# Two of nine interpolation taps transposed by DMA, and sampling one tile later

## The chip, the cores and the metric

The kernel runs on one core of one Trainium2 chip. The metric is the device time of one execution in microseconds; the median of three runs of the kernel before is 2494.78 us (2494.53 to 2497.68).

## The reference

The input is x with shape [4, 128, 64, 64] in float32. Layer 0 is a group norm, an attention over the 4096 pixels of each image with 128 channels, a projection and a residual. Layer 1 is

```python
out = relu(batchnorm(conv2d(x, w1)))              # 3x3
offsets = conv2d(out, w_off) + b_off              # 18 channels: 9 rows, 9 columns
# for each pixel and each of the 9 taps: position = pixel + tap + offset, clipped
# value = bilinear mix of the 4 neighbours of that position
out = batchnorm(conv2d(sampled values, w2))       # one 128x128 matrix per tap
return relu(out + x)
```

## The kernel before, in words

The program is written by hand with one instruction stream per engine and semaphores between them. Helpers: `after(eng, key, n)` waits until the semaphore `key` has counted n steps, and `stored` waits for n transfers of 16 counts. A number in float32 is carried as a sum of two float16 numbers (hi and lo), and `three` (lines 1039 to 1043) makes a product of three float16 matmuls: hi by hi (line 1041), hi by lo (1042) and lo by hi (1043). The attention stage (until about 1600 us of the span) already transposes part of its probabilities by DMA: line 264 issues one transfer of twelve 128x128 blocks per step on the queue of the SyncE engine (SP). Then come conv1, the offset conv (lines 1177 to 1209), and the deformable stage, which the change is about.

The deformable stage works on 128 tiles of 128 pixels (4 images of 32 tiles, a tile is eight patches of 4x4 pixels). `HALF` = 16 tiles make a half image, and TensorE's loop body (line 1265) is one half image. A tile q goes through these steps:

- GpSimd (`interp`, line 451) multiplies row weights and column weights ("hats") into SS, 128 pixels by nine taps by 120 window positions, in float32. SS has two buffers. Its wait is for the transposes of the tile two before.
- TensorE (`interp_transposes`, line 1217) transposes the nine taps, three each into PSUM banks 0 to 2, waiting for VectorE to have emptied the bank.
- ScalarE (`interp_hi`, line 623) copies each bank to STh in float16, laid out patch by patch with the taps side by side, and VectorE (`interp_lo`, line 975) subtracts it from the bank into STl. Both have two buffers.
- SP (line 309) loads for every second tile a window of h1 (`XW`, four buffers) in three transfers of 320 KB, each 10 rows by 4 by 8 KB.
- TensorE (`sample`, line 1225) multiplies for each of the eight patches the window by the weights, three matmuls of 144 columns a patch, in sections of three, three and two patches (banks 3 to 5).
- ScalarE (`sampled`, line 631) and VectorE (`sampled_lo`, line 982) split the result in hi and lo.
- TensorE (`conv2`, line 1237) multiplies it by the weights of the nine taps, 27 matmuls of 128 columns, and VectorE adds it to the output (`z_add`) and takes statistics every fourth tile.

In one turn of TensorE's loop the order is: transposes of tile q, then a section of `sample` for tile q-1 and a third of `conv2` for tile q-2, three times. In tiles 5 and 8 of a half image GpSimd also computes the distances for the next half image (`distances`), and in tiles 10 to 13 ScalarE turns them into hats (`hats`, line 641), between the copies of `interp_hi` and `sampled`. The order on each engine is fixed by the program.

Of the kernel before, what the change touches and what calls it, by code (L numbers as in the profile page):

```python
# [18 lines left out]
F16 = mybir.dt.float16  # L19
I32 = mybir.dt.int32  # L20
ALU = mybir.AluOpType
# [19 lines left out]
TAPS = 9  # L41
# [21 lines left out]
NBUF = 4  # L63
SECT = ((0, 3), (3, 3), (6, 2))
# [30 lines left out]
def build(nc, x, weights, consts, out):  # L95
# [6 lines left out]
    with ctx:  # L102
# [3 lines left out]
        def sb_in(scope, name, shape, dt):  # L106
# [46 lines left out]
        XS = sb_in(l1, "xt_stage", [128, 2, 4, 2 * C], F16)  # L153
        l1a = ExitStack()
        ZT = sb_in(l1a, "zeros_f16", [128, 768], F16)
# [22 lines left out]
        STh = sb_in(l1b, "interpT_hi", [128, 2, 8, TAPS, 16], F16)  # L178
        STl = sb_in(l1b, "interpT_lo", [128, 2, 8, TAPS, 16], F16)
# [29 lines left out]
        s_ld = [sem(f"windows_loaded{i}") for i in range(NBUF)]  # L209
        s_fx = [sem(f"final_loaded{i}") for i in range(B)]  # L210
# [13 lines left out]
            tt="interp_transposed", th="interpT_hi_ready", tl="interpT_lo_ready", mm="sampled",  # L224
# [18 lines left out]
        def _(sp):  # L243
# [57 lines left out]
            for i in range(2):  # L301
                stored(sp, s_xs[i], B * NCH * 2)
            after(sp, "l1", L1_FLAG)
# [5 lines left out]
            with sp.Fori(0, ny) as iy:  # L309
                with sp.Fori(0, nx) as ix:  # L310
                    with sp.Fori(0, B) as b:
                        for i in range(HH // TW):

                            after(sp, "mm", (iy * SX + ix) * (3 * GROUPS) + b * (3 * GPI) + 6 * (i - (NBUF - 1)))
                            row = (iy + sy0) * WR + b * IMG_ROWS + (GUARD + TW * i - 3 - WR * (SY // 2))
                            slot = row * PITCH + (ix + sx0) * (WC // TW) + (0 - (WC // TW) * (SX // 2))
                            for a in range(WC // TW):
                                src = bass.AP(xt_dram.tensor, (slot + a) * (2 * C),
                                              [[PITCH * 2 * C, WR], [SLOTS * 2 * C, TW], [1, WW // TW * 2 * C]])
                                sp.dma_start(XW[WR * TW * a:WR * TW * a + WR * TW, i % NBUF, :, :], src).then_inc(s_ld[i % NBUF], 16)  # L320
# [11 lines left out]
        def _(po):  # L332
            for k in s:
                po.sem_inc(s[k], OPEN)
            for k in s_xo + s_xs + s_tr:
                po.sem_inc(k, OPEN)
# [93 lines left out]
            po.tensor_tensor(SM[:, 12:13], SM[:, 11:12], SM[:, 0:1], ALU.pow).then_inc(s["l1p"], 1)  # L430
            for b in range(B):
# [929 lines left out]
```

## Time and profile before

| what | value |
|---|---|
| median of three runs | 2494.78 us |
| profiled execution | 2493.83 us |
| its span, first to last instruction | 2491.7 us |
| PE (TensorE) busy | 2315.7 us, 93% |
| DVE (VectorE) busy | 1855.8 us, 74% |
| ACT (ScalarE) busy | 1795.1 us, 72% |
| POOL (GpSimd) busy | 1310.9 us, 53% |
| granted TensorE clock over the span | 0.97 |
| first transpose of the deformable stage | 1886.26 us |
| last sampled subtraction of the stage | 2444.47 us |

Busy shares are averages over stages. For the deformable stage the rows below give its own pace. PE is TensorE's matmuls, PEld its weight loads, SPq the queue of SP; L1222 is line 1222.

### The profile page before, as it was taken

To read this page: it belongs to the slowest core of one execution; us is meant where nothing else is said; L and a number is where in the kernel's file an instruction comes from. 1 tells how busy PE (TensorE), PEld (TensorE's weight loads), DVE (VectorE), ACT (ScalarE), POOL (GpSimd) and SP (SyncE) were. 2 spreads that over 40 slices of the span, in tenths; PEclk is the share of its full clock that TensorE was granted. 3 is DMA by queue.
4 is the path that set the end of the run, shared out by engine and by line. 5 is a ranking of instruction groups with operands and counts; after the bars stand their busy time and mean duration, and the time that the engine had idled before them with its cause. 6 is when DMAs were issued, how large, how long until landed. Compare 5 with 4: busy or idle time off the path is not lost.

```text
span 2491.7 us, 73903 instructions
## 1 busy us (share of the span) xinstructions
PE 2315.7 (93%) x27053; PEld 1877.2 (75%) x27053; DVE 1855.8 (74%) x3901; ACT 1795.1 (72%) x2963; POOL 1310.9 (53%) x1067
## 2 busy tenths in 40 slices
PE   5999999999999999999999999799877999899992
PEld 3777777777777777777777777588447999899992
DVE  6778777778877777877777777587666877777875
ACT  5778888878888888888888888532556766666754
POOL 4557545555545555544555555663116665556650
PEclk9999999999999999999999999899898999999996
DMA  3878887778787877877777777771224433333336
GB/s 108 166 144 147 141 162 140 147 149 146 145 159 133 150 145 145 150 129 129 149 147 146 148 146 148 192 235 59 66 71 133 124 113 113 111 111 117 115 95 270
DMA packets 917462, 345.25 MB, mean 139 GB/s; under 512 B 844256, under 2 KB 904160, under 8 KB 909024
## 3 DMA queue, kind: packets, MB, share of 16 engines
q1 hardware_dynamic: 917216, 341.87, 63.6%
q8 instruction: 167, 2.74, 0.5%
q14 instruction: 79, 0.65, 0.1%
HBM read 98.76 MB, written 41.68 MB: 56 GB/s over the span
## 4 chain that ended last, share of the span: by engine, by line
PE 75%; issue 9%; POOL 7%; DVE 4%; DMA 3%; ACT 1%; SPq 1%; POOLq 0%; DVEq 0%; ACTq 0%
PE psum L1041 14%; PE psum L1042 14%; PE psum L1043 14%; POOL probs_split L363 7%; PE psum L1080 7%; PE psum L1082 7%; PE psum L1081 7%; PE psum L1222 5%; PE psum L1066 3%; DMA probsT_dma<-probs_split 1%; PE psum L1195 1%; DMA final<-x_scratch 1%; DVE padded_hi L946 0%; PE psum L1120 0%; PE psum L1203 0%
## 5 line engine op out<-in xcount | busy, mean ns | idle before, releaser
L363 POOL TENSOR_TENSOR probs_split<-probs,probs_split 128x768 f16<-128x768 f32 x512 | 841.8, 1644 | 697.0 <-ACT probs_split L512 696.8
L711 DVE TENSOR_REDUCE neg_max<-psum 128x1 f32<-128x1024 f32 x512 | 626.6, 1224 | 333.0 <-PE psum L1043 332.8
L509 ACT ACTIVATE probs<-psum,exp_bias 128x1024 f32<-128x1024 f32 x512 | 570.2, 1114 | 220.2 <-DVE exp_bias L713 215.6
L1080 PE MATMUL psum<-vT_hi,probsT_dma 128*128 128x129 f16 x3072 | 549.6, 221 | 4.1 <-DMA probsT_dma<-probs_split 4.1
L1082 PE MATMUL psum<-vT_hi,probsT_dma 128*128 128x129 f16 x3072 | 549.5, 219 | 0.0
L1081 PE MATMUL psum<-vT_lo,probsT_dma 128*128 128x128 f16 x3072 | 549.4, 218 | 0.0
L512 ACT ACTIVATE probs_split<-probs 128x768 f16<-128x768 f32 x512 | 431.7, 843 | 22.8 <-ACT probs L509 1.0
L455 POOL TENSOR_TENSOR interp<-row_hats,col_hats 128x360 f32<-128x360 f32 x384 | 294.4, 795 | 219.6 <-PE psum L1222 214.7
L1041 PE MATMUL psum<-k_hi,q_hi 128*128 128x512 f16 x1024 | 387.8, 379 | 3.9 <-DVE q_lo L827 2.4
L1042 PE MATMUL psum<-k_lo,q_hi 128*128 128x512 f16 x1024 | 388.1, 379 | 0.0
L1043 PE MATMUL psum<-k_hi,q_lo 128*128 128x512 f16 x1024 | 388.1, 379 | 0.0
L1081 PEld LDWEIGHTS psum<-vT_lo,probsT_dma 128*128 128x128 f16 x3072 | 302.2, 98 | 0.0
L1080 PEld LDWEIGHTS psum<-vT_hi,probsT_dma 128*128 128x128 f16 x3072 | 297.6, 97 | 5.0 <-DMA probsT_dma<-probs_split 4.9
L1082 PEld LDWEIGHTS psum<-vT_hi,probsT_dma 128*128 128x128 f16 x3072 | 296.1, 96 | 0.0
L980 DVE TENSOR_TENSOR interpT_lo<-psum,interpT_hi 120x384 f16<-120x384 f32 x384 | 191.3, 550 | 89.5 <-ACT interpT_hi L629 88.5
L638 ACT ACTIVATE sampled_hi<-psum 128x432 f16<-128x432 f32 (+1 forms) x384 | 182.3, 495 | 90.0 <-PE psum L1043 89.8
L988 DVE TENSOR_TENSOR sampled_lo<-psum,sampled_hi 128x432 f16<-128x432 f32 (+1 forms) x384 | 207.1, 553 | 51.2 <-ACT sampled_hi L638 46.7
L629 ACT ACTIVATE interpT_hi<-psum 120x384 f16<-120x384 f32 x384 | 162.4, 491 | 92.2 <-PE psum L1222 89.9
L723 DVE TENSOR_TENSOR probsT_lo<-psum,probsT_hi 128x256 f16<-128x256 f32 x512 | 214.0, 418 | 3.1 <-ACT probsT_hi L502 3.1
L1041 PE MATMUL psum<-sampled_hi,weights_hi 128*128 128x128 f16 x1152 | 215.5, 221 | 0.6 <-DVE sampled_lo L988 0.6
L1043 PE MATMUL psum<-sampled_hi,weights_lo 128*128 128x128 f16 x1152 | 214.1, 220 | 0.0
L1042 PE MATMUL psum<-sampled_lo,weights_hi 128*128 128x128 f16 x1152 | 213.8, 220 | 0.0
(181 smaller groups left out, 5532.1 us busy)
## 6 DMA issues: line engine op xcount, KB each, us to landing
xt_windows<-xt_scratch SPq DMA_DIRECT2D x192, 320.0 KB
xt_scratch<-zeros_f SPq DMA_DIRECT2D x28, 576.0 KB, 4.4
probsT_dma<-probs_split SPq DMA_TRANSPOSE x512, 3.7
x_residual<-x SPq DMA_DIRECT2D x128, 64.0 KB, 2.6
x_scratch<-x_out SPq DMA_DIRECT2D x128, 64.0 KB, 2.4
x_rows<-x_scratch SPq DMA_DIRECT2D x32, 256.0 KB, 3.4
xt_scratch<-xt_stage SPq DMA_DIRECT2D x128, 64.0 KB
final<-x_scratch SPq DMA_DIRECT2D x16, 512.0 KB, 10.7
```

The source lines that it names most:

```text
L363: po.tensor_tensor(PH[:, j, 1, :], P[:, j, 0:DW], PH[:, j, 0, :], ALU.subtract).then_inc(s["pl"], 1)
L455: last = po.tensor_tensor(SS[:, g % 2, :, WR * TW * a:WR * TW * a + WR * TW].rearrange("p k (j x) -> p k j x", j=WR), HX[:, hb, g, :, :, N ...
L509: act.activation(P[:, j, :], sc, ACT.Exp, bias=NB[:, par, j:j + 1]).then_inc(s["exp"], 1)
L512: act.activation(PH[:, j, 0, :], P[:, j, 0:DW], ACT.Copy).then_inc(s["ph"], 1)
L711: ve.tensor_reduce(NM[:, par, j:j + 1], sc, AX.X, ALU.max, negate=True).then_inc(s["mx"], 1)
L723: ve.tensor_tensor(PTl[:, k, :, :].rearrange("p m q -> p (m q)"), PS[:, 4 + j % 2, 0:CH - DW], PTh[:, k, :, :].rearrange("p m q -> p (m q) ...
L1041: pe.matmul(dst, lh, rh, start=start, stop=False)
L1042: pe.matmul(dst, lh, rl, start=False, stop=False)
L1043: return pe.matmul(dst, ll, rh, start=False, stop=stop)
L1080: pe.matmul(dst, th, Vh[:, p, v, 0:129], start=n == 0, stop=False)
L1081: pe.matmul(dst[:, 0:128], th, Vl[:, p, v, :], start=False, stop=False)
L1082: last = pe.matmul(dst, tl, Vh[:, p, v, 0:129], start=False, stop=n == KT - 1)
```

## The change

The interpolation taps 0 to 6 are transposed by TensorE, four into PSUM bank 0 and three into bank 1, and copied out by ScalarE and VectorE bank by bank. The taps 7 and 8 don't pass TensorE: ScalarE copies them from SS to SH in float16 (`dma_taps_hi`), VectorE subtracts that from SS (`dma_taps_lo`), and SP transposes the four blocks (two taps, hi and lo, 120 columns padded to 128) with one DMA to the buffer ST that TensorE reads. ST keeps each tap as hi and lo blocks of 128 pixels, and has four buffers in place of two; SH has four. A sample matmul therefore reads its 144 moving columns as nine runs of 16. Sampling of a tile comes two tiles behind its transposes, conv2 three tiles, z_add four. GpSimd's `interp` waits for the VectorE split as well. On SP the two transposes of a tile pair stand between the window loads, and the first image of a pass is written out ahead of the loop over images. The padding of SH is cleared once by GpSimd before the stage, and XS (a buffer of the stage before) moves to make room.

```diff
+DTAP = 2
+PTAP = ((0, 4), (4, 3))
+T0 = TAPS - DTAP
-        STh = sb_in(l1b, "interpT_hi", [128, 2, 8, TAPS, 16], F16)
-        STl = sb_in(l1b, "interpT_lo", [128, 2, 8, TAPS, 16], F16)
+        ST = sb_in(l1b, "interpT", [128, 4, TAPS, 2, 128], F16)
 # SP
+                    def transposed(b, g):
+                        q = (iy * SX + ix) * GROUPS + b * GPI + g
+                        after(sp, "dl", q + 1)
+                        after(sp, "mm", q * 3 - 9)
+                        sp.sem_inc(s_go, 1)
+                        sp.dma_start_transpose(ST[:, g % 4, T0:TAPS, :, :].rearrange("p k e x -> p (k e) x"),
+                                               SH[:, g % 4, :, :, :].rearrange("p k e x -> p (k e x)")).then_inc(s_td[g % 4], 16)
+                    def image_steps(b, first):
                         for i in range(HH // TW):
+                            windows(b, i)
+                            if i or not first:
+                                transposed(b, 2 * i - 2)
+                                transposed(b, 2 * i - 1)
 # GpSimd, interp
-                after(po, "tt", q * 3 - 3)
+                after(po, "tt", q * 2 - 2)
+                after(po, "dl", q - 1)
 # ScalarE
+            def dma_taps_hi(q, g, hid):
+                after(act, "pr", q + 1)
+                stored(act, s_td[g % 4], hid * 4 + g // 4)
+                act.activation(SH[:, g % 4, :, 0, 0:KW], SS[:, g % 2, T0:TAPS, :], ACT.Copy).then_inc(s["dh"], 1)
...
-                        for i in range(3):
+                        dma_taps_hi(q, g, hid)
+                        for i in range(2):
                             interp_hi(q, g, i)
...
-                                sampled(q - 1, (g + 1) % 2, i)
+                                sampled(q - 2, g % 2, i)
 # VectorE
+            def dma_taps_lo(q, g):
+                after(ve, "dh", q + 1)
+                ve.tensor_tensor(SH[:, g % 4, :, 1, 0:KW], SS[:, g % 2, T0:TAPS, :], SH[:, g % 4, :, 0, 0:KW], ALU.subtract).then_inc(s["dl"], 1)
...
+                            dma_taps_lo(q0 + g, g)
+                            for i in range(2):
+                                interp_lo(q0 + g, g, i)
 # TensorE
-                for i in range(3):
-                    after(pe, "tl", q * 3 + (i - 2))
-                    for k in range(3):
-                        last = pe.transpose(PS[0:KW, i, 128 * k:128 * k + 128], SS[:, g % 2, 3 * i + k, :], ident)
+                for i, (k0, nk) in enumerate(PTAP):
+                    after(pe, "tl", q * 2 + (i - 1))
+                    for k in range(nk):
+                        last = pe.transpose(PS[0:KW, i, 128 * k:128 * k + 128], SS[:, g % 2, k0 + k, :], ident)
                     last.then_inc(s["tt"], 1)
...
+                    sh, sl = (ST[0:KW, g % 4, :, e, 16 * t:16 * t + 16] for e in range(2))
+                    dst = PS[:, 3 + i, 144 * (t - t0):144 * (t - t0) + 144].rearrange("p (k x) -> p k x", k=TAPS)
+                    last = three(dst, xw[:, 0:C], xw[:, C:2 * C], sh, sl, True, True)
...
-                                sample(q - 1, p, i)
-                            if g >= 2 or not first:
-                                conv2(q - 2, g % 2, i)
+                                if i == 0:
+                                    pe.wait_ge(s_td[p % 4], (hid * 4 + ((g - 2) // 4 + 1)) * 16 + OPEN)
+                                sample(q - 2, p, i)
+                            if g >= 3 or not first:
+                                conv2(q - 3, (g + 1) % 2, i)
```

## Rows read from the trace of the kernel before

**Rows 1.** The page's head, the span.
```profile
span 2491.7 us, 73903 instructions
```

**Rows 2.** Who TensorE waited for, 1885 to 2455: total us, times, longest.
```profile
PE psum L1222 <- issue: 30.1, 6, 6.6
PE psum L1222 <- POOL interp L455: 14.9, 1, 14.9
```

**Rows 3.** Chain of waits, 1900 to 2492: start us, us, what.
```profile
2088.23 2.17 PE psum L1222 x9
2098.72 0.99 PE psum L1222 x9
2106.73 0.99 PE psum L1222 x9
...
2154.77 6.65 issue
```

**Rows 4.** Timeline, one tile from 2102.56: start, us, engine, line, op, count, [idle before].
```profile
2102.56 1.15 PE L1222 MATMUL psum<-constants,interp 128*120 128x128 f32 x9
2102.70 0.46 DVE L988 TENSOR_TENSOR sampled_lo<-psum,sampled_hi 128x288 f16<-128x288 f32 x1 [0.15 <-ACT sampled_hi L638]
2103.17 1.25 ACT L629 ACTIVATE interpT_hi<-psum 120x384 f16<-120x384 f32 x3 [0.50 <-PE psum L1222]
...
2103.55 0.23 PE L1041 MATMUL psum<-interpT_hi,xt_windows 120*128 120x144 f16 x1
...
2103.79 2.30 POOL L455 TENSOR_TENSOR interp<-row_hats,col_hats 128x360 f32<-128x360 f32 x3 [1.70 <-PE psum L1222]
...
2104.11 0.22 PE L1041 MATMUL psum<-sampled_hi,weights_hi 128*128 128x128 f16 x1
```

**Rows 5.** Timeline of ScalarE, VectorE, TensorE in a tile with hats, 1994 to 1998.
```profile
1994.36 1.75 ACT L647 ACTIVATE col_hats<-col_hats,small 128x1728 f32<-128x1728 f32 x1
1995.98 1.26 ACT L638 ACTIVATE sampled_hi<-psum 128x432 f16<-128x432 f32 x3
...
1996.56 1.49 DVE L988 TENSOR_TENSOR sampled_lo<-psum,sampled_hi 128x432 f16<-128x432 f32 x3 [1.12 <-ACT sampled_hi L638]
...
1998.18 0.22 PE L1041 MATMUL psum<-sampled_hi,weights_hi 128*128 128x128 f16 x1
```

**Rows 6.** Groups by line and shape, 1885 to 2455: total us, mean ns, idle before.
```profile
L988 DVE TENSOR_TENSOR sampled_lo<-psum,sampled_hi 128x288 f16<-128x288 f32 x128 | 58.2, 455 | 15.3 <-ACT sampled_hi L638 15.3
L638 ACT ACTIVATE sampled_hi<-psum 128x288 f16<-128x288 f32 x128 | 53.4, 417 | 34.8 <-PE psum L1043 34.8
```

**Rows 7.** DMA queues and issues, 1920 to 2430.
```profile
DMA packets 8639, 57.34 MB, mean 112 GB/s; under 512 B 1710, under 2 KB 1710, under 8 KB 1710
...
q1 hardware_dynamic: 8550, 56.04, 36.1%
...
xt_windows<-xt_scratch SPq DMA_DIRECT2D x171, 320.0 KB
```

**Rows 8.** DMA queues and issues in attention, 400 to 600; last number us to landing.
```profile
q1 hardware_dynamic: 112179, 29.14, 79.3%
...
probsT_dma<-probs_split SPq DMA_TRANSPOSE x69, 3.7
```

**Rows 9.** Line 264 on the SP queue: duration ns min/median/max.
```profile
L264 SPq DMA_TRANSPOSE probsT_dma<-probs_split x64: 1274/1434/2412, 1001.1 to 1199.9; - x64
```

**Rows 10.** Busy time 1877.5 to 1903.5: PE PEld DVE ACT POOL, clock, DMA share, GB/s.
```profile
1877.50:1903.50 26.00, 17.14 (x205) 16.64 (x205) 12.88 (x27) 16.04 (x29) 18.71 (x22) 0.73 0.61 191
```

**Rows 11.** Weight loads of lines 1185 and 1203: ns min/median/max.
```profile
L1185 PEld LDWEIGHTS psum<-constants,h_rows x128: 195/209/231, 1745.4 to 1860.5; 128*128 128x128 f32 x128
...
L1203 PEld LDWEIGHTS psum<-constants,offset_rows x128: 138/140/231, 1755.7 to 1864.4; 128*128 128x128 f32 x128
```

**Rows 12.** Timeline of GpSimd, and chain of waits, at the start of the stage.
```profile
1883.82 9.27 POOL L455 TENSOR_TENSOR interp<-row_hats,col_hats 128x360 f32<-128x360 f32 x12 [4.78 <-ACT col_hats L650]
...
1896.70 0.98 PE psum L1222 x9
```

More of the change, by code:

```diff
@@ L209, in build @@
         s_ld = [sem(f"windows_loaded{i}") for i in range(NBUF)]
+        s_td = [sem(f"interp_dma_transposed{i}") for i in range(4)]
+        s_go = sem("interp_transpose_released")
         s_fx = [sem(f"final_loaded{i}") for i in range(B)]
@@ L302, in _ @@
                 stored(sp, s_xs[i], B * NCH * 2)
+            sp.wait_ge(s_pz, 11)
             after(sp, "l1", L1_FLAG)
@@ L310, in _, with windows @@
                 with sp.Fori(0, nx) as ix:
-                    with sp.Fori(0, B) as b:
-                        for i in range(HH // TW):
[L314 to L320, printed above, removed]
+                    def windows(b, i):
+                        after(sp, "mm", (iy * SX + ix) * (3 * GROUPS) + b * (3 * GPI) + 6 * (i - (NBUF - 1)))
+                        row = (iy + sy0) * WR + b * IMG_ROWS + (GUARD + TW * i - 3 - WR * (SY // 2))
+                        slot = row * PITCH + (ix + sx0) * (WC // TW) + (0 - (WC // TW) * (SX // 2))
+                        for a in range(WC // TW):
+                            src = bass.AP(xt_dram.tensor, (slot + a) * (2 * C),
+                                          [[PITCH * 2 * C, WR], [SLOTS * 2 * C, TW], [1, WW // TW * 2 * C]])
+                            sp.dma_start(XW[WR * TW * a:WR * TW * a + WR * TW, i % NBUF, :, :], src).then_inc(s_ld[i % NBUF], 16)
@@ L321, in _ @@
+                    image_steps(0, True)
+                    with sp.Fori(1, B) as b:
+                        image_steps(b, False)
+                    transposed(B - 1, GPI - 2)
+                    transposed(B - 1, GPI - 1)
             for i in range(4 * B):
@@ L334, in _ @@
                 po.sem_inc(s[k], OPEN)
-            for k in s_xo + s_xs + s_tr:
+            for k in s_xo + s_xs + s_tr + s_td:
                 po.sem_inc(k, OPEN)
@@ L672, in _ @@
                 half_image(NHALF - 1, 1, False, True)
-                for i in range(3):
-                    sampled(n * GROUPS + (GROUPS - 1), 1, i)
+                for g in range(2):
+                    for i in range(3):
+                        sampled(n * GROUPS + (GROUPS - 2 + g), g, i)
             after(act, "l1", L1_AB2)
@@ L1008, in half_image @@
                         if g < HALF:
-                            for i in range(3):
-                                interp_lo(q0 + g, g, i)
-                        if 3 <= g < HALF + 3:
-                            z_add(q0 + (g - 3), h, g - 3)
-                        elif g < 3 and not first:
-                            z_add(q0 + (g - 3), h - 1, g - 3 + HALF)
-                        if g <= HALF and (g or not first):
-                            for i in range(3):
-                                sampled_lo(q0 + (g - 1), (g + 1) % 2, i)
+                            dma_taps_lo(q0 + g, g)
+                            for i in range(2):
+                                interp_lo(q0 + g, g, i)
+                        if 4 <= g < HALF + 4:
+                            z_add(q0 + (g - 4), h, g - 4)
+                        elif g < 4 and not first:
+                            z_add(q0 + (g - 4), h - 1, g - 4 + HALF)
+                        if g < HALF + 2 and (g >= 2 or not first):
+                            for i in range(3):
+                                sampled_lo(q0 + (g - 2), g % 2, i)
                         if g >= 4 and g % 4 == 3:
@@ L1227, in sample @@
                 if i == 0:
-                    after(pe, "tl", q * 3 + 3)
+                    after(pe, "tl", q * 2 + 2)
                 after(pe, "xl", q * 3 + (i - 2))
```

40 lines of the change are left out of this document (19 added, 21 removed).

## The prediction

> **What bounds the kernel now.** I read the views in this order: who TensorE waited for in the deformable stage, the chain that ended last, one tile of the timeline, one of the tiles in which ScalarE also prepares weights ("hats"), then the DMA queues. The span is 2491.7 us [rows 1]; the stage runs from about 1886 to 2445, 128 tiles. In all of it TensorE waited only 14.9 us for the first interp tile and 30.1 us in six stalls with no releaser ("issue") [rows 2]. The stalls (5.0 us in the mean, up to 6.65) lie at the jumps back of TensorE's loop over half images, and behind each the nine transposes take 2.17 instead of 0.99 us [rows 3]. Between them TensorE is never idle: two tiles take 2106.73 - 2098.72 = 8.01 us, 4.00 each. A tile is 0.99 us of nine transposes (2102.56 to 2103.55), 24 sample matmuls in three pieces, the first piece of nine 0.56 us (to 2104.11), and 27 conv2 matmuls; these 51 take the other 3.01 us [rows 4]. ScalarE's copies, VectorE's subtractions and GpSimd's products (2.30 us of 4.00, then idle 1.70) run in its shadow. So the stage is TensorE's count of instructions times their pace; what leaves TensorE leaves the time, until something in its shadow comes out.
>
> **Part 1, the transposes.** Nine transposes a tile become seven. Each takes 0.99 / 9 = 0.110 us [rows 3], so the tile falls by 0.22 us to 3.78; 128 x 0.22 = **-28.2 us**. The bank waits fall from three a tile to two and are not waited on now [rows 2].
>
> **Part 2, copies of the seven taps.** ScalarE and VectorE handle 512 + 384 columns in two instructions instead of 3 x 384 = 1152 in three, and add one each of 240 columns out of SBUF: 1136 columns, again three instructions. The nearest rows to 240 columns are those of 288, 0.417 us on ScalarE and 0.455 on VectorE [rows 6]; 48 columns fewer are a little less, I take 0.37 and 0.40. Bounds 0.3 and 0.6. Total load is unchanged. The new split of the two taps can run at the tile's start, where ScalarE now idles 0.50 us before its first copy [rows 4]; VectorE waits there too. Cost nothing in ordinary tiles. If VectorE and GpSimd slowed each other here, GpSimd's 1.70 us of idle (1.48 at the new period) covers it. GpSimd's new wait (for the split of the tile two before) is passed about 1.2 us into the tile, where its old one (2103.79 - 2102.56 = 1.23) was [rows 4]; behind it only interp and the distances queue, and TensorE needs the result a whole tile later.
>
> **Part 3, tiles with hats.** In four of 16 tiles ScalarE puts a hat (up to 1.75 us) between the interp copies and the sampled copies. There the shadow is full: the last subtraction ends at 1996.56 + 1.49 = 1998.05 and conv2 reads it at 1998.18 [rows 5]; 0.13 us to spare. Counted from that tile's start (1992.63), the subtraction ends at 5.42. After the change the first copy starts 0.11 later (four transposes, not three, ahead of it), two copies take some 0.25 less than three, so it ends near 5.28; conv2 wants it at 3.78 + 0.77 + 0.56 = 5.11. It is 0.2 to 0.3 late, and the next tile's first copy is up to 0.28 later again, behind the new split. The two column hats pay, the shorter row hats hardly: 0.4 us in each of seven half images with hats, **+3 us** (bounds 0 and 7: nothing, or 0.25 in all 28 such tiles).
>
> **Part 4, the transfer.** Per tile one DMA transpose of four 128x128 blocks. The nearest row is attention's, of twelve blocks (line 264): 79.3% of 16 engines for 200 us is 2538 engine-us for 69 transfers and some copies, about 35 each without the copies; landing 3.7 us after issue [rows 8]. A third is 12 engine-us, 0.75 us over 16 engines. Bounds: 0.7 (a third) and 2.2 us (as much as twelve blocks). Its issue on the SP queue takes at most the 1.43 us of twelve blocks [rows 9]; SP is otherwise idle.
> The windows: 15 transfers took the 26 us of the row, 1.73 each, at 0.61 of 16 engines [rows 10]. The 1710 small packets of 171 transfers are ten for each [rows 7], so each runs on ten engines; 36.1% x 16 x 510 / 171 = 17.2 engine-us over ten is again 1.7. Three per two tiles are 5.2 us. With two transposes 5.2 + 1.5 = 6.7 of 7.56 us: busy, not binding.
> The Trainium skill (DMA: Bandwidth & Descriptors, "Why a DMA increments its semaphore by 16 and not by 1") says that the engine count of a hardware-issued DMA is the largest number up to 16 that divides the slowest dimension of both sides; the window's is ten rows, so ten engines. By that rule the trace agrees, and the transposes, with 128 partitions, would use all 16.
> Latency: the split is ready some 1.2 us into tile q, sampling needs it at 2 x 3.78 + 0.77 = 8.3, so 7.1 us are there. The worse of two transposes is issued one tile behind a window (5.2 us, about 1 us before it starts), lands some 8 us after that window's issue, which is 4.2 to 4.5 us after its own. Slack near 3 us: **0**. The windows' own requests move behind the transposes in SP's order and then come three tiles after a buffer is free, still five tiles before use: 0. SP's new jump between images can hold one transfer back by a stall as in rows 3, and TensorE's own stall lies on the same spot: 0.
>
> **Part 5, the strided moving operand.** Sampling now reads 9 runs of 16 elements, 512 bytes apart, not 144 in a row. The trace has no such matmul. Weight loads show a strided read: the one with every element 16 bytes apart takes 209 ns against 140 [rows 11], 0.54 ns a jump. Bounds: 0, and 9 x 0.54 = 4.9 ns per matmul, x 24 x 128 = 15 us. I take 0: only one element in 16 is a jump, and row and rule below lean there.
> The Trainium skill (SBUF — State Buffer, the note on cachelines under "Door 1: The DMA port swizzle (why [64,N] ≈ [32,N])") says a read is at full rate if it uses each 16-byte line at least twice; runs of 32 bytes do. By its rule the cost is 0; a reader who takes "each access that crosses to a new line pays" literally gets the 15 us.
>
> **Part 6, ends.** At the start sampling begins a tile later, behind three transposed tiles. GpSimd delivers the first four interp tiles by 1883.82 + 9.27 = 1893.09 [rows 12]; before, by 1896.7 TensorE had done three tiles' transposes and two tiles of sampling [rows 12]. Now three transposed and one sampled are done by 1893.6 to 95, and the missing 3.0 us brings it to 1896.6 to 98: **+1 us** (0 to 2). At the end both orders leave one conv2 alone behind VectorE. The six stalls: the instruction fetch now meets more DMA traffic, and spread by 2 us already: **+1 us** (-5 to +7).
>
> **Sum.** -28.2 + 3 + 1 + 1 = -23.2. Span 2491.7 - 23.2 = 2468.5; the execution adds 2493.83 - 2491.7 = 2.1, 2470.6; the median of the runs, 2494.78, lies 0.95 above the profiled execution: 2471.6. Within 0.2% (5 us) counts as no change.
>
> **Rivals.**
> A, forecast: TensorE-bound tiles of 3.78 us, 2462 to 2481; 0.63.
> B, strided reads cost TensorE up to 4.9 ns a matmul: tile 3.9, gain 8 to 17 us, 2483 in the middle of it. For: rows 11. Against: one jump in 16. 0.13.
> C, the DMA engines become the bound, so TensorE waits for the transposed taps ahead of sampling. Place: ten engines shared by windows and transposes. It decides when 5.2 + 2X exceeds 7.56 (X over 1.2 us) and makes the kernel slower when 5.2 + 2X exceeds 8.0 (X over 1.4). With X = 1.8, between the third and the full row, a tile is 4.4 us: +0.4 x 128 = +51, 2546. For: ten engines at 5.2 us, short packets. Against: attention's 35 engine-us for twelve blocks. 0.12.
> D, the hats and the new order cost more: each late copy moves the next tile (ScalarE's new split queues behind sampled copies, and VectorE, GpSimd behind it). If the shadow holds every tile at about 3.95 us, only 6 us are gained: 2489. For: 0.13 us of margin in hat tiles. Against: in the other 12 of 16 tiles the last subtraction ends at 2102.70 + 0.46 = 2103.16 and conv2 starts at 2104.11 [rows 4], 0.95 us of margin. 0.08.
> E, no gain because the stalls grow by about 4 us each: 6 x 4 eats the gain, 2495. 0.04.
>
> Faster takes A, B, and most of D: 0.81. Same 0.06: E and part of D. Slower 0.13: C and a tail. Range: below A's low end little; C is left out above: 2460 to 2496.
>
> **What would show it.** Right: chain with x7 transposes of 0.77 us every 3.78 us; sample matmuls of unchanged spacing (0.56 us for nine); TensorE waiting for DMA nowhere; waits of 0.2 to 0.4 us on VectorE's sampled subtraction after column hats. Wrong: nine sample matmuls in 0.60 us (B); TensorE waiting for the interp DMA, with issue to landing above 7 us (C); periods of 3.9 us all over with TensorE idle before sampling or conv2 (D); "issue" stalls near 9 us (E).

## The result, and the profile after

The changed kernel takes 2524.66 us (median of four runs, 2520.51 to 2525.37) where the kernel before takes 2494.66 (four runs, 2493.39 to 2497.68): 1.0115 times as long, interval 1.0098 to 1.0133. It is slower by 30 us; the forecast was 2471.6, faster by 23. The profiled execution took 2520.51 us, its span is 2518.5 (2491.7 before, [rows 1]).

Who TensorE waited for in the stage, 1880 to 2480 (total us, times, longest), which answers to [rows 2]. L1261 is the transposes, L1080 the first matmul of three:

```profile
PE psum L1261 <- issue: 40.3, 6, 9.4
PE psum L1080 <- DMA interpT<-interp_split: 17.3, 20, 2.4
PE psum L1261 <- POOL interp L482: 14.9, 1, 14.9
PE psum L1080 <- DVE sampled_lo L1026: 9.0, 13, 1.0
PE psum L1261 <- DVE interpT L1017: 1.7, 2, 0.9
PE psum L1080 <- DVE interpT L1017: 1.7, 1, 1.7
```

Before there were two lines of any size, the stalls at the loop's jumps (30.1) and the first tile (14.9). Now TensorE waits for the new transfer twenty times ahead of sampling, for VectorE thirteen times, and the six stalls are 10 us longer. The chain of waits from 1880 to the end (start us, us, what) shows both at once; its largest share by line is the transfer, 17.0%, and "issue" has 13.3%:

```profile
1984.68 7.78 DMA interpT<-interp_split
...
2012.71 0.77 PE psum L1261 x7
...
2016.50 8.56 issue
2025.06 1.75 PE psum L1261 x7
...
2064.69 11.70 DMA interpT<-interp_split
...
2311.54 9.41 issue
```

The DMA queues and issues of 1920 to 2430, against [rows 7]:

```profile
DMA packets 68737, 70.92 MB, mean 139 GB/s; under 512 B 61923, under 2 KB 61923, under 8 KB 61923
...
q1 hardware_dynamic: 68643, 69.59, 89.2%
...
xt_windows<-xt_scratch SPq DMA_DIRECT2D x167, 320.0 KB
interpT<-interp_split SPq DMA_TRANSPOSE x112, 4.6
```

36.1% of sixteen engines has become 89.2%, for 24% more bytes. One cycle of two tiles, in the timeline (start, us, engine, line, op, count, [idle before]); first TensorE's part of it, then the SP queue's:

```profile
2111.86 0.93 PE L1261 MATMUL psum<-constants,interp 128*120 128x128 f32 x7
...
2115.65 0.93 PE L1261 MATMUL psum<-constants,interp 128*120 128x128 f32 x7
2117.35 0.23 PE L1080 MATMUL psum<-interpT,xt_windows 120*128 120x144 f16 x1 [0.77 <-DMA interpT<-interp_split]
...
2124.16 0.93 PE L1261 MATMUL psum<-constants,interp 128*120 128x128 f32 x7
...
2125.68 0.23 PE L1080 MATMUL psum<-interpT,xt_windows 120*128 120x144 f16 x1 [0.58 <-DMA interpT<-interp_split]
...
2107.50 1.26 SPq L324 DMA_DIRECT2D xt_windows<-xt_scratch  x3
2109.18 4.98 SPq L331 DMA_TRANSPOSE interpT<-interp_split  x2
2114.52 2.29 SPq L324 DMA_DIRECT2D xt_windows<-xt_scratch  x3
2118.39 4.63 SPq L331 DMA_TRANSPOSE interpT<-interp_split  x2
2123.39 1.27 SPq L324 DMA_DIRECT2D xt_windows<-xt_scratch  x3
```

The reader is to see two things. A tile that waits for nothing takes 2115.65 - 2111.86 = 3.79 us, as forecast (3.78); the two that follow take 2124.16 - 2115.65 = 8.51, with a wait of 0.77 us in them for the transfer that was issued at 2109.18. And the even transfer of a pair, the first one behind the windows, is the late one. The next even one, that of the tile of 2115.65, is issued at 2118.39, behind the windows of 2114.52, and lands 7.07 us later, at 2125.46, where TensorE has waited for it since 2125.10. For all 128 the trace gives the issue, and for 96 the landing too:

```profile
L331 SPq DMA_TRANSPOSE interpT<-interp_split x128: 1188/1198/2258, 1890.5 to 2462.2; - x128
...
DMA to landing us min/median/max: 2.4/4.5/11.7
```

Taken apart, the even ones take 7.1 us in the median (32 landings on record), the odd ones 4.1 (64).

Busy time in stretches (PE PEld DVE ACT POOL, clock, DMA share, GB/s): 45 us without a jump, then the three half microseconds in which the transfer issued at 2102.80 runs with the queue to itself, and two stretches in which the queue nearly stands still:

```profile
2102.00:2147.00 45.00, 42.23 (x637) 41.21 (x636) 38.56 (x81) 31.31 (x70) 31.35 (x36) 1.00 0.93 140
...
2104.00:2104.50 0.50, 0.50 (x11) 0.50 (x8) 0.50 (x3) 0.50 (x2) 0.50 (x2) 1.00 0.98 198
2104.50:2105.00 0.50, 0.50 (x7) 0.50 (x6) 0.50 (x3) 0.19 (x1) 0.49 (x1) 1.00 0.31 62
2105.00:2105.50 0.50, 0.50 (x11) 0.49 (x8) 0.50 (x3) 0.48 (x1) 0.00 (x0) 1.00 0.17 33
...
2115.50:2116.70 1.20, 1.08 (x13) 0.84 (x10) 1.05 (x3) 0.87 (x3) 1.20 (x1) 1.00 0.27 26
2123.60:2125.10 1.50, 1.50 (x20) 1.25 (x17) 1.32 (x4) 0.70 (x2) 0.17 (x1) 1.00 1.46 22
```

The same 45 us of the kernel before:

```profile
2102.00:2147.00 45.00, 45.00 (x677) 44.88 (x675) 37.12 (x81) 34.50 (x71) 31.07 (x36) 1.00 0.43 127
```

Alone a transfer is (0.98 + 0.31 + 0.17) x 0.5 x 16 = 11.7 engine-us and lands in 2.4 us: the forecast's 12. TensorE is busy 42.23 us of 45, before in all of them. The last two rows of the first block are not idle time of the queue: by the packet records 23 packets that begin from 2115.3 to 2115.8 end from 2116.7 to 2117.1, and 21 that begin at 2123.7 end at 2125.1; meanwhile 22 to 26 GB/s move, where the 45 us have 140.

**Where the span's 26.8 us lie.** 3.1 lie ahead of the stage (first transpose at 1889.39, before at 1886.26); in the profiled executions of all the kernels below this point lies anywhere from 1884.9 to 1893.1, so these 3.1 need not be the change's. From first to last tile's first transpose it is 571.7 us against 550.9, +20.9; the rest, 2.8, follows the last transposes, where sampling of one more tile is left, as it was left out at the start. I count the intervals from one tile's first transpose to the next. Before, 113 of them are below 5.6 us and sum to 452.4 (4.00 each); the 13 others, at and behind the jumps, to 98.5. After, 114 sum to 462.9 (4.06 each) and 13 to 108.9. (Before, the first two tiles follow within a microsecond and count as one, so it has one interval less, worth 3.8.) At 3.78 the 114 would be 430.9: **32 us are lost in ordinary tiles and 10 at the jumps**, against the 24.9 that shorter tiles save there (113 x 0.22); -24.9 + 32.0 + 10.4 + 3.8 is the 20.9 within 0.4. Of the 32 the rows of waits name 28 (DMA 17.3, VectorE 9.0 and 1.7).

The share of VectorE in this is smaller than its lines say. A wait with several conditions is put down to the one that was met last. In the 13 waits ahead of sampling that have VectorE's name (12 on `sampled_lo`, one on `interpT`; 10.2 us), the transfer that the same matmul needs had landed only 0.04 to 0.26 us before VectorE was done. Without VectorE TensorE would still have waited some 26 us for late transfers.

### The profile page after: what moved, and what is told of

It is laid out like the page before. It is cut to its first block, busy times and chain, and to the rows that moved or that the text cites. A ratio compares the mean times of both kernels' runs of the same rounds, so it can differ in the third digit from the quotient of the medians.

```text
span 2518.5 us, 75085 instructions
## 1 busy us (share of the span) xinstructions
PE 2300.8 (91%) x26797; PEld 1849.1 (73%) x26797; DVE 1867.6 (74%) x3901; ACT 1794.3 (71%) x2963; POOL 1312.1 (52%) x1068
## 4 chain that ended last, share of the span: by engine, by line
PE 65%; issue 11%; POOL 7%; DMA 7%; DVE 5%; ACT 2%; SPq 1%; POOLq 0%; DVEq 0%; ACTq 0%
PE psum L1080 13%; PE psum L1082 12%; PE psum L1081 12%; POOL probs_split L388 7%; PE psum L1119 7%; PE psum L1121 7%; PE psum L1120 7%; DMA interpT<-interp_split 4%; PE psum L1105 3%; PE psum L1261 2%; DMA probsT_dma<-probs_split 1%; PE psum L1234 1%; DMA final<-x_scratch 1%; DVE sampled_lo L1026 1%; DVE padded_hi L980 0%
## 5 line engine op out<-in xcount | busy, mean ns | idle before, releaser
L1080 PE MATMUL psum<-k_hi,q_hi 128*128 128x512 f16 x1024 | 388.1, 379 | 3.6 <-DVE q_lo L861 2.4
L1080 PE MATMUL psum<-interpT,xt_windows 120*128 120x144 f16 x1024 | 212.7, 231 | 28.5 <-DMA interpT<-interp_split 17.3
L1080 PE MATMUL psum<-sampled_hi,weights_hi 128*128 128x128 f16 x1152 | 217.3, 222 | 0.9 <-DVE sampled_lo L1026 0.6
L1082 PE MATMUL psum<-interpT,xt_windows 120*128 120x144 f16 x1024 | 211.0, 229 | 0.0
```

What stands on the lines that cost most here:

```text
L1080: pe.matmul(dst, lh, rh, start=start, stop=False)
L1082: return pe.matmul(dst, ll, rh, start=False, stop=stop)
```

## The experiments

The theories at the outset: T, throughput (windows and transfers together need more of the DMA engines than the tiles give); L, latency (the transfer behind the windows lands too late, the queue itself has room); J, the jumps (more traffic makes the stalls at TensorE's jumps longer, as an instruction fetch would that waits in it); S, the strided reads or the new order of ScalarE and VectorE cost the time. Later Q: the queue's need isn't a sum over its transfers but depends on their order. Each kernel is a change of the kernel after unless it says otherwise; each was timed beside the kernel before on the same chip (its median 2494.2 to 2495.5), and ratios are to that.

One measure goes through all of them. The engine time of the queue from 1920 to 2430 is its share x 16 x 510; I take 17.2 for each window transfer [rows 7] and put the rest on the transposes in the stretch (nowin is read from 1920 to 2380, as it writes its output behind that). The share adds up the times of packets, which can overlap (lag3 and split pass 100%), so it tells how long packets take, those that are held included, rather than how full an engine is. It also charges to the transposes what the window packets take longer: in the kernel after 0.49 us each against 0.43, some 4 of the 39.3.

| kernel | us | ratio (95%) | DMA share | engine-us per transpose | landing, median |
|---|---|---|---|---|---|
| nowin | 2453.17 | 0.9829 (0.9813 to 0.9846) | 18.4% | 11.9 | 2.5 |
| spread | 2483.11 | 0.9965 (0.9952 to 0.9978) | 77.1% | 27.3 | 3.9 |
| together | 2496.04 | 1.0002 (0.9992 to 1.0013) | 84.6% | 32.9 | 5.1 |
| lag3_spread | 2492.2 | 0.9991 (0.9981 to 1.0001) | 90.4% | 37.0 | 5.1 |
| after | 2524.66 | 1.0115 (1.0098 to 1.0133) | 89.2% | 39.3 | 4.5 |
| lag3 | 2528.56 | 1.0122 (1.0106 to 1.0139) | 101.7% | 49.3 | 8.5 |

**nowin: no windows.** Only the first four window buffers are loaded; the other windows of the input are left out.

```diff
-                            windows(b, i)
+                            if first and i < NBUF:
+                                windows(b, i)
```

(and TensorE's wait for a window asks only for the first load of its buffer)

> The changed kernel, with the windows loaded only for the first four tile pairs (later tiles read old windows, so this part of the input is left out). Theory T, throughput: in the changed kernel the ten DMA engines are busy without a break, a window 5.2 us and two transposes 1.55 us each, 8.3 us a pair, which is the measured pair (3.79 + 4.5 us). Without windows every tile takes 3.79 us and the whole comes to 2470 to 2475. Theory L, latency: the queue has time to spare, but every second transpose stands behind a window and lands 7.2 us after its issue; it also gives 3.79 us here. Theory S: the strided moving reads or the new order of ScalarE and VectorE cost the time; then tiles stay above 4 us and the time above 2510. Theory J, stalls at the loop's jump grow by DMA traffic: the six stalls, 40.3 us in sum with the change and 30.1 before, fall to 25 to 30.

Measured 2453.17 us (2453.01 to 2458.6), 20 us below what T and L both said. TensorE's waits, and the queue:

```profile
PE psum L1262 <- issue: 17.4, 6, 3.0
...
PE psum L1081 <- DMA interpT<-interp_split: 1.2, 1, 1.2
```

```profile
interpT<-interp_split SPq DMA_TRANSPOSE x120, 2.5
```

Tiles take 3.79 us, transfers land in 2.5, and one wait for DMA is left. So the transposes and the new order do what the forecast said of them; the loss needs the windows beside the transfers. Whether it needs both in one queue no run shows. The expectation missed the size because the stalls fell to 17.4 us. Eight of 120 regular intervals still exceed 4.2 us, and all together they are 7.9 us above 3.787 each. About half of that, 3.7 us, lies in tile 8 of the half images, right behind VectorE's slowest split, which runs beside GpSimd's distances (start, us, engine, line):

```profile
1977.09 2.44 DVE L1012 TENSOR_TENSOR interp_split<-interp,interp_split 128x240 f16<-128x240 f32 x1
...
1976.14 3.13 POOL L473 TENSOR_TENSOR col_hats<-constants,offsets 128x1728 f32<-128x1728 f32 x1
```

In 111 tiles the split takes 0.40 us in the mean; in the 17 that overlap an instruction of GpSimd it takes 1.75, mostly 1.42 or 2.44. Tile 8 costs 3.2 us in pe9_dma, which has the split, and nothing in pe9, which has none. The tiles behind the hats (12 and 14) cost 2.3.

**pe9: no transfer.** All nine taps by TensorE; ST with its strided reads and sampling two tiles behind stay.

```diff
-PTAP = ((0, 4), (4, 3))
+PTAP = ((0, 3), (3, 3), (6, 3))
```

(and dma_taps_hi, dma_taps_lo and transposed are taken out, with their waits)

> The changed kernel with all nine taps transposed by TensorE again (three banks of three), no split and no transfer of the two taps; the new layout of ST with its strided moving reads, four buffers and sampling two tiles behind stay. T and L: tiles of 4.00 us, 2494 to 2498. S: above 2505, with nine sample matmuls in more than 0.56 us.

Measured 2481.66 us (2477.59 to 2486.28), 0.9938 (0.9921 to 0.9955): 13 us faster than before where no change was expected.

```profile
PE psum L1253 <- issue: 17.3, 6, 3.2
...
PE psum L1072 <- issue: 11.3, 6, 3.4
```

Its tiles take 4.00 us each (2102.63, 2106.63, 2110.64), as before, and its sample matmuls follow each other every 62 ns, as before: reading 144 moving columns as nine runs of 16 costs nothing, and S falls. The stalls come in two pieces, one ahead of the transposes and one ahead of sampling, 28.6 us in all.

**pe9_lag1: pe9 with sampling one tile behind**, to see where those 13 us come from.

```diff
-                                sample(q - 2, p, i)
+                                sample(q - 1, p, i)
```

(conv2, z_add and their waits move with it)

> pe9 (no transfer, all nine taps by TensorE, 2481.7 us, 13 us faster than the kernel before at the same 4.00 us a tile) with sampling one tile behind again; what is left of the change is ST's layout and its four buffers. If the tile more between transposes and sampling makes the stalls at the jump cheaper (in pe9 they come in two pieces, 17.3 and 11.3 us, where before it was one of 30.1): 2492 to 2497. If the layout or the buffers do it: 2480 to 2484.

Measured 2496.03 us (nine runs of 2494.34 to 2498.16 and one of 2539.86), 1.0005 (0.9995 to 1.0015), stalls of 29.1 us in one piece. The gain belongs to the extra tile of lag. The stalls' sums are near each other (30.1, 29.1, 28.6); what differs is the work around them. The intervals around the jumps are longer than 4.004 us each by 44.2 us in sum in the kernel before, 44.0 in pe9_lag1 and 35.8 in pe9. These 8.4 us are more than the 7.6 by which the profiled executions of before and pe9 differ.

**pe9_dma: pe9, and the transfer runs all the same** into a buffer that nobody reads, so nothing waits for it.

```diff
-                        sp.dma_start_transpose(ST[:, g % 4, T0:TAPS, :, :]...
+                        sp.dma_start_transpose(SD[:, g % 4, :, :, :]...
```

> As pe9, but the split and the transfer of taps 7 and 8 are made as well, into a buffer that nobody reads or waits for. So the DMA traffic of the change is there, and no engine but SP depends on it. T: the queue needs 8.3 us a pair and TensorE only 8.0, so the window loads fall behind and TensorE waits for them in the end: 2505 to 2520. L: nobody waits for a late transpose, tiles stay at 4.00: 2495 to 2500. J: the six stalls stay near 40 us here, and are near 30 in pe9.

Measured 2503.9 us (2497.98 to 2506.96), 1.003 (1.0019 to 1.0041): 22 us above pe9.

```profile
q1 hardware_dynamic: 70799, 71.47, 78.9%
...
unread<-interp_split SPq DMA_TRANSPOSE x115, 4.0
```

Tiles stay at 4.00 us but for tile 8 of each half image, behind GpSimd's distances (4.46). Of the 19.5 us by which the profiled execution is above pe9's (2505.77 and 2486.28), some 14 lie in the intervals around the jumps. The stalls themselves are 30.8 us in sum and not the 40 that J expected (28.6 in pe9), so most of the 14 lie in what runs around a stall. That DMA traffic costs time at the jumps is seen here without any wait for data; how it does is not.

**split: more engines for the windows.** Each window transfer becomes one of 32 partitions and one of 8, in the hope that 16 and 8 engines do what ten did.

```diff
+                            for r0, nr in ((0, 32), (32, 8)):
```

(cut: the addresses of the two pieces, and TensorE's wait counts six transfers for three)

> The changed kernel, with each window transfer of 40 rows made as one of 32 rows and one of 8, so that 16 engines take part in the first and eight in the second: the busiest engines carry 9 rows of 8 KB per window instead of 12, 3.9 instead of 5.2 us. T: 3.9 + 3.1 = 7.0 us a pair, below TensorE's 7.56, so tiles of 3.79 and 2470 to 2480. L: the transpose behind a window lands 1.3 us earlier, which is most of what TensorE waits: 2475 to 2490. If the count of engines has nothing to do with it: 2520 to 2530.

Measured 2578.84 us (2572.22 to 2584.61), 1.0337 (1.0311 to 1.0364), the worst of all, where a gain was expected.

```profile
PE psum L1082 <- DMA interpT<-interp_split: 28.9, 23, 2.3
PE psum L1082 <- DVE interpT L1019: 28.3, 14, 2.4
```

By the packet records an 8 KB packet takes 0.73 us here and 0.49 in the kernel after: each went slower. The nine packets that the busiest engine has of a whole window would take 6.6 us in a row, the twelve of the kernel after 5.9. All 28.3 us on VectorE's copy stand beside a late transfer too: it had landed at most 0.3 us before the copy ended. The expectation was wrong in taking the number of engines for what sets a window's time. It also speaks against plain T with a fixed work per transfer. The edit doubles the number of window transfers as well, and this wasn't separated from the number of engines.

**spread: the same transfers in another order.** Two of a window's three transfers go ahead of the first transpose of a pair, the third ahead of the second.

```diff
-                            windows(b, i)
+                            windows(b, i, range(2))
                             if i or not first:
                                 transposed(b, 2 * i - 2)
+                            windows(b, i, range(2, 3))
+                            if i or not first:
                                 transposed(b, 2 * i - 1)
```

> The changed kernel with one edit in SP's order: of the three transfers of a window two are issued ahead of the first transpose of the pair and the third ahead of the second, where all three stood ahead of the first. The bytes and the number of transfers are the same. Theory L (latency: the transpose behind the whole window lands 7.2 us after its issue and some 9.8 us after its tile began, where sampling needs it at 8.3): it stands behind two thirds of a window, lands 1.7 us earlier, in time; tiles near 3.79 but for the hats, 2485 to 2500, the long stalls at the loop's jump staying. Theory T (throughput: the queue needs 8.3 us a pair): no change, 2520 to 2528.

Measured 2483.11 us (2478.69 to 2492.56), 0.9965 (0.9952 to 0.9978): 41.5 us below the kernel after.

```profile
PE psum L1263 <- issue: 26.6, 6, 7.1
...
PE psum L1082 <- DMA interpT<-interp_split: 5.7, 7, 1.5
```

Waits for the transfer fall from 17.3 to 5.7 us, stalls from 40.3 to 26.6, and the queue carries its 320 KB windows and transposes in 77.1% where it took 89.2%. Bytes, packets and engines are the same.

**lag3: more time for the transfer.** Sampling comes three tiles behind, so a transfer may take 3.8 us longer.

```diff
-                                sample(q - 2, p, i)
+                                sample(q - 3, p, i)
```

(conv2, z_add, the statistics and their waits move with it)

> The changed kernel with sampling three tiles behind the transposes (conv2 four, z_add five) instead of two; transfers, buffers and SP's order as they were. L: a late transpose has one tile more, 12.1 us from its tile's start; TensorE waits for no transfer in the steady part: tiles near 3.79 but for the hats, 2485 to 2500. T: TensorE still waits, 2518 to 2528.

Measured 2528.56 us (2522.41 to 2531.09), 1.0122 (1.0106 to 1.0139). L said the waits would go and falls:

```profile
q1 hardware_dynamic: 67816, 68.39, 101.7%
...
interpT<-interp_split SPq DMA_TRANSPOSE x110, 8.9
```

The transfers take the added time and more, 8.9 us to landing, and TensorE still waits 13.5 us for them, and 8.8 in five waits on VectorE's copy, in which the transfer had landed at most 0.25 us before the copy was done. So the queue is behind: time alone doesn't bring it back.

**lag3_spread: both.** The edits of lag3 and spread.

> Both edits, lag3 and spread, together. L: nothing left for the second to cure, within 3 us of the faster of the two alone. T: 2518 to 2528.

Measured 2492.2 us (2489.7 to 2501.23), 0.9991 (0.9981 to 1.0001). One wait of 0.3 us for DMA is left, but the stalls are 37.6 us. No wait for the transfer, and still 9 us slower than spread, where L had said within 3: the stalls are 11 us longer than spread's 26.6, at 90.4% of DMA against 77.1%.

**together: a second order.** As lag3, but the first transpose of a pair waits for the second's split, so that both are issued back to back behind one window and none runs alone.

```diff
-                        after(sp, "dl", q + 1)
+                        after(sp, "dl", q + (1 + more))
...
-                                transposed(b, 2 * i - 2)
+                                transposed(b, 2 * i - 2, 1)
```

> lag3 with one more wait on SP: the first transpose of a pair is issued only when the second one's split is ready too, so both stand in the queue right behind each other, and the window that is issued behind them has a whole pair's time to drain; no transpose stands behind a window. Bytes and transfers are those of lag3 (2528.6 us). Theory Q (the queue's need for a pair depends on the order: a transpose behind a whole window costs more than its own 0.75 us, since the six free engines run ahead and the ten of the window finish it late): tiles near 3.79, 2485 to 2500, landing near 4 us. Theory T (the queue needs over 7.6 us a pair in any order of the same bytes; spread would then have won by something else): 2515 to 2530.

Measured 2496.04 us (2489.42 to 2500.45), 1.0002 (0.9992 to 1.0013): 32 us below lag3 with the same transfers, although each first transpose starts later. Waits for DMA 2.7 us (13.5 in lag3), stalls 40.5 (40.3). This is Q's case; a fixed work per transfer would have given lag3's time, 2515 to 2530 by T.

**before_nowin: the kernel before without the windows** (as in nowin, the windows beyond the first four pairs of tiles are left out).

> The kernel before, with the windows loaded only for the first four tile pairs (this part of the input is left out, as in nowin). TensorE never waited for a window, so its tiles stay at 4.00. Theory J (the stalls at the jump grow by DMA traffic): they fall from 30 us to about 17 and the time to 2475 to 2483; nowin, at 2453, is then 22 to 30 us below it, the transposes' whole price. If the stalls owe nothing to the windows: 2493 to 2496.

Measured 2485.71 us (2482.14 to 2488.35), 0.9959 (0.9945 to 0.9973); tiles 4.00, stalls 22.1 us where they were 30.1 (J had said about 17). Even the traffic of before costs 8 us at the jumps.

**dtap1 and dtap1_spread: one tap by DMA.** Eight taps by TensorE, two blocks in the transfer; the second with spread's order.

```diff
-DTAP = 2
-PTAP = ((0, 4), (4, 3))
+DTAP = 1
+PTAP = ((0, 4), (4, 4))
```

> The changed kernel with one tap by DMA (two blocks) and eight by TensorE (two banks of four); SP's order as in the change. TensorE: 4.00 - 0.11 = 3.89 us a tile. T and Q: half the transposed bytes, the queue needs 5.2 + about 1.5 us of 7.8 a pair and keeps up, TensorE waits for no transfer in the steady part; 2485 to 2498, depending on the stalls at the jump. If a transpose costs the same whatever its size, TensorE still waits: 2515 or more.

> dtap1 and spread together. Tiles of 3.89 us and little traffic at the jump: 2475 to 2485; if it beats both spread (2483.1) and pe9 (2481.7) it is the best of the versions.

Measured 2494.49 us (2486.07 to 2500.83), 0.9997 (0.9984 to 1.0009), and 2485.34 (2481.2 to 2486.59), 0.9959 (0.9945 to 0.9973). Tiles take 3.89 us, and waits for DMA are 0.7 and 1.7 us. The queue:

```profile
q1 hardware_dynamic: 42472, 65.58, 50.9%
...
interpT<-interp_split SPq DMA_TRANSPOSE x118, 4.4
```

By the measure above a transfer of two blocks costs 9.8 engine-us, one of four blocks 39.3: twice the blocks, four times the cost. In spread's order it is 11.7 against 27.3, 2.3 times. The queue is no longer a limit, yet of 128 x 0.11 = 14 us nothing is seen against before: with pe9's 13 us from the lag, 27 should be. The regular intervals of dtap1 are 11.9 us above 3.894 each, nearly all of it in tile 8 (3.4) and behind the hats in tiles 10, 12 and 14 (6.9). Of TensorE's waits 4.7 us (nine) are on sampled subtractions, and here they are VectorE's own: in the eight ahead of sampling the transfer had landed over 8 us before. The stalls are 31.1; the rest is open. Dtap1_spread doesn't beat spread or pe9.

**before_flat, after_flat, spread_flat: no jumps.** TensorE's loop over half images is written out.

```diff
-                with pe.Fori(1, NHALF) as h:
+                for h in range(1, NHALF):
                     half_image(h, range(HALF), False)
```

> The kernel before with TensorE's loop over half images written out flat. If the six turns around the jump (30.1 us of stall and some 14 of slow matmuls behind them) are the jump's alone: 2450 to 2456. If other engines stall at their own loops at the same place: 2465 to 2485.

> The changed kernel with the same edit. If the growth of the stalls (30.1 to 40.3 us) is an instruction fetch that waits in DMA traffic: it falls by more than before_flat does, by 50 us and up, to 2475 or less, unless the queue, which caught up during the stalls, now makes TensorE wait more (theory Q: a transpose behind a window): then 2480 to 2500, with over 20 us of waits for the transposes.

> spread with the same edit: steady tiles near 3.79 but for the hats, no jump: 2435 to 2450, and below before_flat by 8 to 20 us, which is then the worth of transposing two taps by DMA with a queue in the right order. If the loops of the other engines stall it as much: 2455 to 2475.

Measured: before_flat 2455.83 us (2455.11 to 2456.44), 0.9842 (0.9825 to 0.9858); after_flat 2482.34 (2474.84 to 2489.65), 0.9952 (0.9934 to 0.997); spread_flat 2466.81 (2457.96 to 2469.33), 0.9881 (0.9854 to 0.9908). TensorE's waits in before_flat, and in after_flat:

```profile
PE psum L1222 <- POOL interp L455: 14.9, 1, 14.9
PE psum L1222 <- DVE interpT_lo L980: 3.6, 2, 1.8
PE psum L1041 <- DVE sampled_lo L988: 0.7, 2, 0.5
```

```profile
PE psum L1080 <- DMA interpT<-interp_split: 14.7, 18, 2.5
PE psum L1261 <- DVE interpT L1017: 8.9, 4, 3.8
PE psum L1080 <- DVE interpT L1017: 6.8, 5, 1.6
PE psum L1080 <- DVE sampled_lo L1026: 6.3, 8, 1.2
```

All "issue" lines are gone, and with them 39 us of before, 42 of after, 16 of spread. Without jumps the change is still 26.5 us slower than its counterpart, nearly the whole 30. So the loss doesn't depend on TensorE's jumps: without them it stands as waits for the transfer, and for VectorE beside it. Two of the waits for VectorE, 3.8 and 3.3 us ahead of transposes, are the jump of another engine: the chain leads them back to "issue" stalls of 6.9 and 5.5 us that end at ScalarE's line 702, its loop over half images. After_flat's time lies in the range that went with Q, though its waits for the transfer are 14.7 us and not over 20, and spread_flat missed 2435 to 2450. And before_flat, which has none of the change in it, is the fastest kernel that computes all: 39 us below the kernel before. With spread's order (spread_flat) the change is 11 us slower than that.

## Why the prediction was wrong

**What failed is part 4**, "With two transposes 5.2 + 1.5 = 6.7 of 7.56 us: busy, not binding", with its "lands some 8 us after that window's issue, which is 4.2 to 4.5 us after its own. Slack near 3 us". Measured: 10.9 us after that window's issue (2114.52 to 2125.46), 7.07 after its own, slack gone, and a pair of tiles takes 8.5 us where it does and not 7.56. In the median an even transfer is issued 1.74 us into its tile (1.2 was forecast) and lands 7.1 us later (4.2 to 4.5 forecast), at 8.9, where sampling needs it at 8.3. So of the slack near 3 us the late issue took 0.5 and the long transfer 2.7 or so, and more than all was gone. The terms were right one by one: 11.7 engine-us and 2.4 us for a transfer alone, 5.2 us for windows alone. Their sum was not. Beside windows the same transfer is charged 27 to 49 engine-us, by order and lag; order alone was worth 41.5 us (spread against after) and 32 (together against lag3). I had even the row for that price, attention's 35 engine-us for twelve blocks [rows 8], and took a third of it. Charged per transfer, 35 lies near the 39.3 that was measured, but that would have been luck: alone the transfer costs 11.7, and two blocks beside windows cost 9.8.

**Of the rivals C was right in place and too high in price.** Its formula, 5.2 + 2X, gives X = 1.65 for a pair of 8.5 us, between its bounds of 0.7 and 2.2; the mean regular tile is 4.06 and not 4.4, as not every pair is late: 69 of 114 intervals lie below 3.9 us and 35 above 4.2. What it called the signs came true: TensorE waits for the interp DMA, with issue to landing above 7 us. But a fixed X is not what spread, together and split show. The rival asked for a chance well above 0.12: the windows alone held 5.2 of 7.56 us, and of the bounds of X, 0.7 to 2.2, two thirds (above 1.2) made C the case.

**Part 1 right.** Seven transposes take 0.77 us in the chain (2012.71), and an undisturbed tile 3.79.

**Part 2 right in ordinary tiles, wrong beside GpSimd's distances.** Nowin's ordinary tiles at 3.79 leave no cost for the copies; ScalarE's takes 0.40 us (0.37 forecast), VectorE's split 0.40 (0.40 forecast). But "If VectorE and GpSimd slowed each other here, GpSimd's 1.70 us of idle (1.48 at the new period) covers it" looked at GpSimd's side alone: beside the distances VectorE's split takes up to 2.5 us, over the bound of 0.6, and tile 8 pays 3 to 4 us in sum, a term that the forecast put at nothing.

**Part 3 about right.** The tiles behind the hats cost 2.3 us in nowin, 3 were forecast. VectorE's 9.0 us in thirteen waits of the kernel after are not this term, since late transfers stand beside twelve of them.

**Part 5 right**, rival B falls: pe9's tile is 4.00.

**Part 6 near on the ends, wrong on the stalls.** For the ends +1 was forecast. Up to the start of tile 4 the stage is 1.4 us shorter than before and behind the last transposes 2.8 longer; as five shorter tiles give 1.1 of this back, the ends cost 2.4. +1 (-5 to +7) was forecast, +10 measured (40.3 against 30.1, single stalls of 3.8 to 9.4 us). That traffic lengthens them was right and the size was not (22.1 in before_nowin, 30.1 at 36.1% of the engines, 40.3 at 89.2%); that it does so through the instruction fetch no run shows. Of rival E, priced at 24 us, less than half came true in this way. The stalls do not follow the share alone: nowin has 17.4 at 18.4%, together 40.5 at 84.6%, pe9_dma 30.8 in two pieces at 78.9%.

**What stays open** is what happens inside the queue. The packet records of the kernel after show packets that are held. Its small packets of 256 bytes take 18 ns in the median and 47 in the mean, and its packets of 4 bytes, 13 ns each in the kernel before, take 255 in the mean. The transfer issued at 2118.39 shows one way: 186 of its 256-byte packets start from 2119.5 to 2120.5 beside the windows, then none for 1.5 us in which ten window packets are in flight at all times and five small ones are held; the rest start from 2122.2, when the windows are done. That fits Q, a transfer that runs ahead on the engines without windows and is finished late by the others. But then comes the stretch of 1.4 us from 2123.7 in which nearly nothing moves, with no window packet in flight, and Q doesn't explain that. From 1920 to 2380 I count 63 stretches of 0.3 us and more with at least eight packets in flight and under 60 GB/s, 58 us in sum; in spread they are 25 with 20 us, in the kernel before none. Together has 53 with 58 us and is fast, so their sum doesn't give the time either. No run took these mechanisms apart, as a second queue for the transposes might. Open too is why one more tile of lag makes the work around the jumps cheaper, worth 13 us in pe9.

## What to carry to other kernels

Work moved from a saturated engine to DMA has to be priced in the queue that it joins, at the nearest row measured beside other traffic and in the order of issue; the time of a transfer by itself was only the lower end, and here the same bytes in another order were 42 us apart. If added latency (one more tile of lag) doesn't remove a wait, the queue is behind and only its order or its load helps. Before trading work between engines, look at the stalls that no releaser explains: writing out one loop gave 39 us, more than the change was forecast to bring.

## What the runs showed of the hardware

- A transfer to 40 partitions did not get faster by being cut in 32 and 8: its 8 KB packets took 0.73 us instead of 0.49, and the kernel 54 us more.
- A DMA transpose of four 128x128 float16 blocks lands in 2.4 us alone and in 7.1 (median) behind 960 KB of windows; its issue keeps SP 1.20 us. Beside windows two blocks cost a quarter of its engine time in one order (9.8 against 39.3 engine-us) and 0.43 of it in another (11.7 against 27.3).
- Beside windows and transposes the queue had stretches of up to 1.5 us with over 20 packets in flight and 22 to 26 GB/s.
- A subtraction of VectorE with both inputs in SBUF (128x240 float32) took 0.40 us, and 1.42 or 2.44 when it ran beside one of GpSimd's instructions of 2.7 to 3.1 us.
- A jump back of TensorE's loop cost 4.4 to 6.7 us before, 3.8 to 9.4 with 89% of DMA, and 3.0 at most with 18%; six of them and what ran slowly behind them were 39 us of 2495.
- A moving operand in runs of 16 float16 (32 bytes), 512 bytes apart, ran at the pace of one in a row.
